# A decoder layer in f32 on one core: PE's waits on one semaphore merged, and the bf16 products put first in the transposed 64-key scores

## The reference

```python
x = x + nystrom_attention(layernorm(x))                  # 16 heads of 16, 64 landmarks
x = x + cross_attention(layernorm(x), ctx_1024, mask)    # 64 keys a batch element
x = x + expert_ffn(layernorm(x))                         # one of 8 experts a batch element

# the attention of the first line, for each head:
q_l, k_l = q.reshape(64, 8, 16).mean(1), k.reshape(64, 8, 16).mean(1)   # q is scaled
attn1 = softmax(q @ k_l.T)       # 512 x 64
attn2 = softmax(q_l @ k_l.T)     # 64 x 64
attn3 = softmax(q_l @ k.T)       # 64 x 512
V = attn2
for _ in range(6):
    KV = attn2 @ V
    V = 0.25 * V @ (13 * I - KV @ (15 * I - KV @ (7 * I - KV)))
out = attn1 @ (V @ (attn3 @ v))

# the attention of the second line, for each head:
ctx = softmax(where(mask == 0, -1e9, Q @ K.T / 4)) @ V   # 512 x 64
```

## Time and profile before

| | us |
|---|---|
| median of 3 runs | 1419.36 |
| the three runs | 1419.16, 1419.36, 2244.75 |
| the profiled execution | 1421.52 |
| its span, first to last instruction | 1419.8 |
| PE busy with products | 1369.3 (96% of the span) |
| DVE busy | 1032.9 (73%) |
| ACT busy | 666.6 (47%) |
| POOL busy | 569.9 (40%) |

### The profile page before, as it was taken

One profiled execution on the slowest core, in us unless ns is written; L12 is line 12 of the kernel. 1 busy time (PEld: TensorE's weight loads), 2 busy tenths in 40 slices (PEclk: granted clock), 3 DMA queues, 4 the chain that ended last, 5 costly groups with the idle time before them and its releaser, 6 DMA issues.

```text
span 1419.8 us, 53827 instructions
## 1 busy us (share of the span) xinstructions
PE 1369.3 (96%) x23732; PEld 896.7 (63%) x23732; DVE 1032.9 (73%) x2194; ACT 666.6 (47%) x1230; POOL 569.9 (40%) x799
## 2 busy tenths in 40 slices
PE   6998999999999999999999999999999999999998
PEld 4756656655666666666666656666675656566555
DVE  2487877848677786867778686777878776898661
ACT  2423355354454545445454545545455453535652
POOL 6223444443615335361533526143352531516223
PEclk9999999999999999999999999999999999999999
DMA  8002010110101001010100101010010100001032
GB/s 281 1 3 91 5 62 3 44 66 11 57 12 51 19 30 39 3 57 12 50 19 19 51 3 57 12 51 18 15 55 4 51 3 19 18 4 37 3 97 64
DMA packets 40538, 53.19 MB, mean 37 GB/s; under 512 B 9699, under 2 KB 30451, under 8 KB 40307
## 3 DMA queue, kind: packets, MB, share of 16 engines
q1 hardware_dynamic: 31602, 41.37, 9.2%
q10 hardware_dynamic: 8704, 8.39, 1.7%
HBM read 37.16 MB, written 12.59 MB: 35 GB/s over the span
## 4 chain that ended last, share of the span: by engine, by line
PE 89%; DVE 4%; issue 2%; ACT 2%; DMA 1%; POOL 1%; DVEq 0%; SPq 0%; POOLq 0%; ACTq 0%
PE bank L1312 41%; PE bank L1555 8%; PE bank L1321 7%; PE bank L1331 7%; PE bank L1542 4%; PE bank L1381 2%; PE bank L1510 2%; PE bank L1446 2%; PE bank L1402 2%; PE bank L1435 2%; PE bank L1523 2%; PE bank L1369 1%; PE bank L1461 1%; PE bank L1408 1%; PE bank L1544 1%
## 5 line engine op out<-in xcount | busy, mean ns | idle before, releaser
L768 POOL TENSOR_TENSOR b<-ut,eye 128x256 f32<-128x256 f32 x192 | 137.2, 730 | 517.2 <-DVE ut L1151 445.2
L930 ACT ACTIVATE az<-bank 128x320 f32<-128x320 f32 x192 | 67.5, 400 | 191.6 <-PE bank L1321 191.2
L1208 DVE RECIPROCAL oT_x<-bank 128x256 f32<-128x256 f32 x64 | 109.3, 1734 | 22.5 <-PE bank L1555 22.5
L1312 PE MATMUL bank<-xnT_a,wqkv 128*128 128x512 f32 x256 | 123.6, 609 | 0.3 <-ACT xnT_a L854 0.3
L1312 PE MATMUL bank<-xnT_c,w1e 128*128 128x512 f32 x256 | 118.7, 605 | 3.0 <-DMA b1e<-in_b 3.0
L1208 DVE RECIPROCAL oT<-bank 128x256 f32<-128x256 f32 x64 | 111.5, 1747 | 10.4 <-PE bank L1555 10.3
L1312 PE MATMUL bank<-w2e,hT 128*128 128x256 f32 x512 | 117.3, 383 | 0.9 <-ACT hT L996 0.9
L1080 DVE TENSOR_REDUCE m<-bank 128x1 f32<-128x512 f32 x128 | 82.9, 680 | 39.4 <-PE bank L1402 37.9
L886 ACT ACTIVATE p3T<-bank 128x512 f32<-128x512 f32 x128 | 66.7, 604 | 83.4 <-PE bank L1435 83.4
L1312 PEld LDWEIGHTS bank<-w2e,hT 128*128 128x128 f32 x512 | 94.9, 190 | 15.2 <-issue 1.7
L1142 DVE SCALAR_TENSOR_TENSOR wb<-bank,eye 128x256 f32<-128x256 f32 x192 | 73.2, 411 | 33.0 <-PE bank L1321 32.3
(11 more groups left out here) (223 smaller groups left out, 3005.0 us busy)
## 6 DMA issues: line engine op xcount, KB each, us to landing
x_in<-in_x SPq DMA_DIRECT2D x16, 512.0 KB, 3.9
w1e<-in_W SPq DMA_DIRECT2D x16, 512.0 KB, 3.6
w2e<-w2o SPq DMA_DIRECT2D x16, 512.0 KB, 4.0
out<-base ACTq DMA_DIRECT2D x32, 256.0 KB, 2.2
row_e<-w2o_row SPq DMA_DIRECT2D x16, 128.0 KB, 4.5
hT<-in_W2T SPq DMA_DIRECT2D x2, 512.0 KB, 6.5
pT_x<-in_ctxT SPq DMA_DIRECT2D x1, 1024.0 KB
ctxT<-in_ctxT SPq DMA_DIRECT2D x16, 64.0 KB, 2.4
```

Of the source, the lines that this page charges most:

```text
L768: return g.tensor_tensor(b7[:, q, :], ut[:, q, :], eye[28 if it else 7][:].unsqueeze(1) .broadcast_to([P, 4, LM]), ALU.subtract).then_inc( ...
L1208: return v.reciprocal(oT[x][:, k, cols], tile(i, ("den" + x, k))[:, cols]).then_inc(dve_done, 1)
L1312: last = mm(dst, lhsT, rhs, start=(k == 0), stop=(k == len(pairs) - 1))
```

## The change

Two things are changed, both in the part of the program that PE runs.

The waits: a step of PE gathers the numbers that its empty banks need by engine (`emptied`), and takes them together with the numbers that its operands need, so that it waits at most once for DVE and once for ACT (`due`). `OPERANDS_FROM` says for which kinds of step an operand wait will follow; for the others the bank's wait stands alone. In steps that wait for both engines the order of the two is set anew. A step still waits for all that it waited for. Of 1041 places where PE waits at the head of a step (after the first few steps), 427 held no instruction of their own that only waits, before or after; 288 keep one; 159 go from two to one, 138 from one to none, 27 from two to none and 2 from three to one. PE's list has 453 such instructions instead of 808.

The products: in t1 and tx the four bf16 products come first and open each bank's accumulation, and the four f32 products close it. Each was the other way round.

The order of steps, the banks, and the lists of the other engines stay as they are. Line numbers move: L1321, L1331, L1446 and L1555 become L1331, L1341, L1462 and L1575, and the two products of t1 and tx are now L1562 (bf16) and L1564 (f32).

```diff
@@ -305,6 +305,11 @@
     return None
 
 
+OPERANDS_FROM = {"q": "A", "k": "A", "v": "A", "s3": "A", "x2T": "D", "mT3": "D", "t3": "AD", "zT": "AD", "z": "A",
+                 "a": "AD", "iT": "AD", "iZ": "AD", "jT": "AD", "jZ": "AD", "y": "D", "s1": "A", "sx": "A",
+                 "mT1": "D", "mTx": "D", "t1": "A", "tx": "A", "den1": "A", "denx": "A", "o1": "AD", "ox": "AD",
+                 "w1": "D", "wx": "D", "qx": "A", "gate": "A", "logit": "A", "h": "A", "y3": "A", "xnTc": "A"}
+
 FUSED = EXPERTS + 1
 
 
@@ -496,6 +501,11 @@
         def unmet(eng, who, i, *steps):
 
             n = max(DONE[who, i, s] for s in steps) if i >= 0 else 0
+            return n if first(eng, done[who], n) else 0
+
+        def due(eng, who, emptied, i, *steps):
+
+            n = max(emptied[who], *[DONE[who, i, s] for s in steps])
             return n if first(eng, done[who], n) else 0
 
         def tile(i, step, j=0):
@@ -1340,11 +1350,17 @@
 
             def body(i, step):
                 kind, n = step[0], step[1] if len(step) > 1 else 0
+                emptied = {"A": 0, "D": 0}
                 for j in range(banks_of(step)):
                     if BEFORE[i, step, j]:
                         who, i0, emptier = BEFORE[i, step, j]
-                        if c := unmet(pe, who, i0, emptier):
-                            pe.wait_ge(done[who], c)
+                        emptied[who] = max(emptied[who], DONE[who, i0, emptier])
+                if "D" not in OPERANDS_FROM.get(kind, ""):
+                    if first(pe, dve_done, emptied["D"]):
+                        pe.wait_ge(dve_done, emptied["D"])
+                if "A" not in OPERANDS_FROM.get(kind, ""):
+                    if first(pe, act_done, emptied["A"]):
+                        pe.wait_ge(act_done, emptied["A"])
                 o = tile(i, step)
                 if kind == "kx":
                     all_consts(pe)
...
                 elif kind == "zT":
-                    if c := unmet(pe, "A", i, *[("e3", n, j) for j in range(4)]):
+                    if c := due(pe, "D", emptied, i, ("v", 0), ("v", 1)):
+                        pe.wait_ge(dve_done, c)
+                    if c := due(pe, "A", emptied, i, *[("e3", n, j) for j in range(4)]):
                         pe.wait_ge(act_done, c)
-                    if c := unmet(pe, "D", i, ("v", 0), ("v", 1)):
-                        pe.wait_ge(dve_done, c)
...
                 elif kind in ("iT", "iZ"):
                     it = n
                     if it:
-                        if c := unmet(pe, "D", i, ("uz", it - 1, 0), ("uz", it - 1, 1)):
+                        if first(pe, act_done, emptied["A"]):
+                            pe.wait_ge(act_done, emptied["A"])
+                        ready = [("uz", it - 1, 0), ("uz", it - 1, 1)]
+                        if kind == "iZ":
+                            ready += [("ut", it - 1, 0), ("ut", it - 1, 1)]
+                        if c := due(pe, "D", emptied, i, *ready):
                             pe.wait_ge(dve_done, c)
                     else:
-                        if c := unmet(pe, "A", i, ("a", 0), ("a", 1)):
+                        if kind == "iZ":
+                            if c := due(pe, "D", emptied, i, ("z",)):
+                                pe.wait_ge(dve_done, c)
+                        elif first(pe, dve_done, emptied["D"]):
+                            pe.wait_ge(dve_done, emptied["D"])
+                        if c := due(pe, "A", emptied, i, ("a", 0), ("a", 1)):
                             pe.wait_ge(act_done, c)
                     if kind == "iT":
                         if c := unmet(pe, "G", i, ("b7", it, 0), ("b7", it, 1)):
                             pe.wait_ge(pool_done, c)
                         last = spread_out(i, step, uz, b7, LM, 0, LM)
                     else:
-                        if it:
-                            if c := unmet(pe, "D", i, ("ut", it - 1, 0), ("ut", it - 1, 1)):
-                                pe.wait_ge(dve_done, c)
-                        else:
-                            if c := unmet(pe, "D", i, ("z",)):
-                                pe.wait_ge(dve_done, c)
                         last = spread_out(i, step, ut, uz, LM + DH, 0 if it < ITERS - 1 else LM, LM + DH)
                 elif kind in ("jT", "jZ"):
                     it = n
-                    if c := unmet(pe, "D", i, ("wb", it, 0), ("wb", it, 1)):
+                    if c := due(pe, "D", emptied, i, ("wb", it, 0), ("wb", it, 1)):
                         pe.wait_ge(dve_done, c)
-                    if c := unmet(pe, "A", i, ("az", it, 0), ("az", it, 1)):
+                    if c := due(pe, "A", emptied, i, ("az", it, 0), ("az", it, 1)):
                         pe.wait_ge(act_done, c)
                     if kind == "jT":
                         last = bring_home(i, step, az, wb, LM, 0, LM)
                     else:
                         last = bring_home(i, step, wb, az, LM + DH, 0 if it < ITERS - 1 else LM, LM + DH)
...
                     keys, query = (kbd, qT) if x == "1" else (kx_bd, qxT)
                     if c := unmet(pe, "G", 0, ("cst",)):
                         pe.wait_ge(pool_done, c)
-                    if c := unmet(pe, "A", i, ("mT" + x,), ("q" if x == "1" else "qx", n)):
+                    if c := due(pe, "A", emptied, i, ("mT" + x,), ("q" if x == "1" else "qx", n)):
                         pe.wait_ge(act_done, c)
                     if c := unmet(pe, "G", i, ("kbd",) if x == "1" else ("kxbd",)):
                         pe.wait_ge(pool_done, c)
                     for j in range(4):
-                        mm(tile(i, step, j)[:], flat(keys[rows(j), n]), query[rows(j), n, :], start=True, stop=False)
+                        mm(tile(i, step, j)[:], flat(minus[rows(j), n]), mT[x][rows(j), :], start=True, stop=False)
                     for j in range(4):
-                        last = mm(tile(i, step, j)[:], flat(minus[rows(j), n]), mT[x][rows(j), :],
+                        last = mm(tile(i, step, j)[:], flat(keys[rows(j), n]), query[rows(j), n, :],
                                   start=False, stop=True)
                 elif kind in ("den1", "denx", "o1", "ox"):
                     x = kind[-1]
-                    if c := unmet(pe, "A", i, *[("e" + x, n, j) for j in range(4)]):
+                    if kind[0] == "o":
+                        if c := due(pe, "D", emptied, i, ("y",) if x == "1" else ("vx",)):
+                            pe.wait_ge(dve_done, c)
+                    if c := due(pe, "A", emptied, i, *[("e" + x, n, j) for j in range(4)]):
                         pe.wait_ge(act_done, c)
-                    if kind[0] == "o":
-                        if c := unmet(pe, "D", i, ("y",) if x == "1" else ("vx",)):
-                            pe.wait_ge(dve_done, c)
                     for j in range(4):
                         w = ones_bd[:] if kind[0] == "d" else (y_bd if x == "1" else vx_bd)[:, 4 * n + j, :]
                         last = mm(o[rows(j), :], w, pT[x][:, 4 * n + j, :], start=True, stop=True)
...
```

More of the change, by code:

```diff
@@ L1396, in body @@
                 elif kind == "s3":
+                    if c := due(pe, "A", emptied, i, ("k", n)):
+                        pe.wait_ge(act_done, c)
                     if c := unmet(pe, "G", i, ("qbd",)):
                         pe.wait_ge(pool_done, c)
-                    if c := unmet(pe, "A", i, ("k", n)):
-                        pe.wait_ge(act_done, c)
                     for j in range(4):
@@ L1415, in body @@
                 elif kind == "mT3":
-                    if c := unmet(pe, "D", i, ("mp3",)):
+                    if c := due(pe, "D", emptied, i, ("mp3",)):
                         pe.wait_ge(dve_done, c)
@@ L1503, in body @@
                 elif kind == "s1":
-                    if c := unmet(pe, "A", i, ("q", n)):
+                    if c := due(pe, "A", emptied, i, ("q", n)):
                         pe.wait_ge(act_done, c)
@@ L1512, in body @@
                 elif kind == "sx":
-                    if c := unmet(pe, "A", i, ("qx", n)):
+                    if c := due(pe, "A", emptied, i, ("qx", n)):
                         pe.wait_ge(act_done, c)
@@ L1526, in body @@
                     x = kind[-1]
-                    if c := unmet(pe, "D", i, ("mp" + x,)):
+                    if c := due(pe, "D", emptied, i, ("mp" + x,)):
                         pe.wait_ge(dve_done, c)
@@ L1585, in body @@
                         pe.wait_ge(expert_out_loaded, 32 * (i + 1))
-                    if c := unmet(pe, "A", i, *[("h", f) for f in range(FM)]):
+                    if c := due(pe, "A", emptied, i, *[("h", f) for f in range(FM)]):
                         pe.wait_ge(act_done, c)
```

36 lines of the change are left out of this document (18 added, 18 removed).

## The result

| | us |
|---|---|
| before, 6 runs beside it | 1419.26 (1417.69 to 1421.84, and one of 2244.75) |
| changed, 6 runs | 1398.59 (1395.74 to 1399.86) |
| ratio | 0.9837, 95% interval 0.9822 to 0.9852 |
| profiled execution of the changed kernel | 1397.8, span 1396.1 |

The change saves 20.7 us where 10 were forecast. 1398.6 lies under the range's lower end of 1402. It lies in the case that the prediction called rival 3, "more borders than I count are late", which had a chance of 0.09.

What follows compares the result with a forecast made beforehand. The prediction took PE's list to bound the kernel. Waits 7.4 us and products 3.8 us made 11.2, less 1.2 for borders becoming late: 10 us, so 1419.4 becomes 1409.4 us, range 1402 to 1417.5.

Steps and rivals of the forecast that it cites:

- rival 3: At PE's step borders: more late waits than counted, sum 17 us, at the far end 28; 1392 to 1405 us, chance 0.09.
- What bounds the kernel: Whole kernel: PE's list sets the time from end to end, with PE busy 96% of the span.
- The price of a late wait: At PE's step borders: a late standalone wait costs 0.06 us and a second one 0.11 more.
- The step on jT: In jT: DVE's late wait moves onto the weight load; behind t1, 12 borders gain 0.17 us each, 2.0 us.
- The count of late borders: At PE's step borders: 12 and 10 in jT, 36 zT/den1/o1/w1, 30 estimated single places; together 7.4 us.
- The products: In t1 and tx: bf16 first shortens a step by 0.09 us, kept in 42 of 64 steps, 3.8 us.
- rival 4: In t1 and tx: f32 loads start only after the bf16 products, costing 11 us; 1423 us, chance 0.05.
- The give-back of 1.2 us: At borders just in time today: they become late when PE comes sooner, taking 1.2 us off the gain.

Runs made afterwards that it cites:

- e2: The kernel before with only the new product order in t1 and tx (bf16 first), all waits as they were; 1416.5 us, ratio 0.9969.
- e5: The changed kernel with always satisfied waits in the 326 places where a standalone wait went away, so PE's list has its old length; 1402.3 us, ratio 0.9871.
- e1: The changed kernel with the products of t1 and tx back in the old order, so only the wait merging is left; 1400.9 us, ratio 0.9856.
- e6: The changed kernel with a satisfied wait called first in every PE step, so all other waits stand alone; 1419.2 us, ratio 0.9995.
- e7: The changed kernel with 368 more standalone waits, all early, in iT, iZ, jT and jZ; 1404.4 us, ratio 0.9907.
- e9: The kernel before with bf16 products first and waits merged in jT and jZ alone, filled to the old list length; 1413.6 us, ratio 0.9949.
- e14: The kernel before with bf16 products first and waits merged in iT and iZ alone, filled to the old list length; 1418.0 us, ratio 0.9965.
- e15: The changed kernel filled to the old list length, but iT and iZ keep separate waits on the emptied bank; 1403.4 us, ratio 0.9859.
- e8: The kernel before with 72 always satisfied waits added at the start, moving what follows in PE's list; 1421.7 us, ratio 0.9999.
- e11: The changed kernel with 232 always satisfied waits added at the start, moving what follows in PE's list; 1400.8 us, ratio 0.9883.

## Why the prediction was wrong, point by point

**What bounds the kernel**: right. PE is 97% busy, and the time that went from its list went from the kernel; no other engine took it over.

**The price of a late wait**: right. 0.06, 0.12 and 0.23 us came from the earlier trace rows; the records give 42 ns for a wait that rides, and 104 and 214 for one and two that stand alone. The description ahead of the prediction had one thing the wrong way round, though, where it says that the last of a step's waits rides on the weight load: the wait that is called first rides, and the later ones become standalone instructions. The step on jT (DVE's wait goes on the load) holds all the same, since DVE's is called first there now that the emptied bank's is gone.

**The count of late borders: this is the step that failed.** The prediction priced 12 + 10 + 36 + 30 = 88 borders, 7.4 us, and wrote: "the wait rows name so few late borders that I stay near the first count". 177 borders stood behind a late standalone wait, and their price was 16.7 us; 5.6 are left in the changed kernel, so 11.1 went. With the list held at its old length, from e2 to e5, 13.9 went. The missing ones repeat in nearly every turn: iT or iZ behind a chain of products 10 times, t1 or tx behind t3 or s1 19 times, jT or jZ behind den, ox or t1 32 times where 22 were counted, xnTb behind a and t3 behind s1 9 times each. About 50 of all had the 0.23 us of two instructions, not 22. The waits list of before doesn't name them as what they are. A border of this kind in the timeline of before, at 394 us:

```profile
393.77 1.17 PE L1510 MATMUL bank<-kbd,qT 32*128 32x128 f32 x32
...
394.01 0.68 DVE L1072 TENSOR_TENSOR vt<-bank,bv_row 128x512 f32<-128x512 f32 x1
...
394.92 0.34 PEld L1542 LDWEIGHTS bank<-qxT,kx_bd 32*128 32x128 f32 x8 [0.17 <-issue]
```

DVE ends at 394.69 and the load starts at 394.92, the 0.23 us of two standalone waits. But the product ahead runs to 394.94, so PE counts as busy, and the load's idle time is put down to issue. The prediction took names from the list where it should have taken the distances of 0.12 and 0.23 from the timeline of one whole turn. It also took the earlier trace rows at its word with 22 waits for wb, though the earlier trace rows shows one under the name of az. Its own upper bound, 355 x 0.06 = 21, was nearer to the 16 to 17 us that the waits gave than its 7.4.

**The supply of the list: a term that the prediction lacked, and the second step that failed.** Issue fell from 7.4 to 0.9 us. The prediction put this at nothing, although has "issue 2%". Of the 20 us this is 6.5 by the two profiles, but it belongs to where the edges of 256 fall, not to the edit: the kernel before has 4.6 to 8.4 us of it by its alignment alone, the changed one 0.9 to 4.3. Between the filled list and the changed kernel, levelled, it was 1.6. So the supply's share of this gain lies between 1.6 and 6.5 us, and the late borders have the larger one.

**The products**: right. 3.8 us forecast, 3.0 and 3.7 measured; the rest column has 1394.3 to 1397.3 for the four kernels with the f32 products first and 1389.9 to 1393.7 for the others, a mean of 1395.3 against 1391.5. The first f32 load now lies under the bf16 products, so rival 4 is out: it needed an f32 start of over 0.44 us after the opening, and it is 0.22.

**The give-back of 1.2 us**: neither shown nor ruled out. Where the products alone came sooner, borders rose by 1.6 us (before to e2) and 1.5 (e1 to changed), which would fit, but such sums are hardly exact to that. If it is there, the 3.0 and 3.7 us above are what is left after it.

**The sum.** The levelled gain of 19.9 us is 6.5 issue, 11.1 borders and 2.3 rest. That it adds up proves nothing, as the rest is what is left over. The rise of the mean clock from 0.9949 to 0.9976 comes on top, 3.9 us by the plain means, and no term of the prediction had it. One part isn't split further: the wait for the expert's b1e at 292 us took 3.0 us in the profile of before and 0.4 in that of the changed kernel, in others 0.0 to 4.0 without order, and it lies in the rest.

## What to carry to other kernels

Where a step waits for several semaphores, the one that comes late should be on the instruction that does the work, and two numbers of one semaphore belong in one wait: here each late wait that stood alone cost 62 ns, a second behind it 110 more, and an early one nothing that could be measured. Count late borders by their distance from the event, over one whole period, not by the names in a list of waits, since under overlapping products they are booked as busy time and as issue. And before an edit is priced that changes the length of an engine's list, look for stops in the middle of a step: they move when anything ahead is added or taken away, and a few us of a comparison can be that alone.

## What the runs showed of the hardware

- PE's instructions arrive in packets of 16.4 KB, and PE can run dry: nine stops of 0.20 to 2.04 us at record 193 or 194 of a block of 256 in the kernel before, 15 of up to 2.81 us, 9.5 us together, in e6, and four of at most 0.30 in the changed kernel.
- The granted clock falls to 0.5, the lower of its two levels, for short pieces, 0 to 4 of 3.4 or 6.8 us within a profile. The kernel before had one at 293 us, right behind PE's stand of 2.5 us for b1e, and one at 1174 while PE was busy. In five kernels (e5, e7, e9, e14, e15) one begins 0.4 to 1.7 us after the stop at about 195 us has ended, in others with the same stop (before, e2, e6, e8) none does. The profiled runs of e1 and e11 had none before their last microseconds.
